# An attention stage in a fused four-layer kernel: keys turned by blocks on VectorE, rotary work on GpSimd, row sums divided out of the output

## The reference

```python
q = rmsnorm(x @ Wq.T).reshape(8, 128, 32, 128)   # 32 query heads, D = 128
k = rmsnorm(x @ Wk.T).reshape(8, 128, 8, 128)    # 8 key heads; each serves 4 query heads
v = (x @ Wv.T).reshape(8, 128, 8, 128)
q, k = rope(q, pos), rope(k, pos)                # halves swapped, times cos and sin
kc, vc = k_cache[block_table], v_cache[block_table]     # 512 cached keys per sequence
p = softmax(q . concat(kc, k) * scale + mask)    # 640 keys per query
x = x + (p @ concat(vc, v)) @ Wo.T
```

## Time and profile before

| | |
|---|---|
| profiled execution, own time | 1516.57 us |
| its span | 1514.8 us (so 1.8 us lie around the span) |
| TensorE matmuls busy | 1422.5 us (94%), 8068 |
| VectorE busy | 1151.0 us (76%), 2779 |
| ScalarE busy | 995.2 us (66%), 1985 |
| GpSimd busy | 495.5 us (33%), 684 |
| mean granted TensorE clock | 0.98 of full speed (2.4 GHz) |
| chain that ended last | TensorE 79% of the span, VectorE 6%, issue 6%, ScalarE 4%, DMA 3% |
| chain, the key transposes L1370 | 2% |
| chain, `attend` L1334 | 13% |

### The profile page before, as it was taken

The page is one execution under the profiler, slowest core; times in us unless marked ns, Lnnn a source line. Parts: engine busy times, 40 slices in busy tenths (PEclk is TensorE's granted clock), DMA queues, the critical chain, the costliest instruction groups (busy, mean ns, idle before and its releaser), DMA issues.

```text
span 1514.8 us, 29533 instructions
## 1 busy us (share of the span) xinstructions
PE 1422.5 (94%) x8068; PEld 1222.2 (81%) x8068; DVE 1151.0 (76%) x2779; ACT 995.2 (66%) x1985; POOL 495.5 (33%) x684
## 2 busy tenths in 40 slices
PE   6989987789999999999999999999999999999888
PEld 4767765678888788888888888888788888888767
DVE  3876666467788788878878887888788878888756
ACT  4756554356677677767767776677677767777643
POOL 5321220144443333334333333333333334333200
PEclk9999999989999999999999999999999999999999
DMA  8885763334321111211211211021111111101214
GB/s 172 299 254 154 220 196 103 112 87 133 113 70 43 51 39 53 61 41 50 62 48 33 71 43 51 29 70 43 51 39 53 61 41 50 63 29 35 98 65 158
DMA packets 103342, 130.47 MB, mean 86 GB/s; under 512 B 11973, under 2 KB 78662, under 8 KB 97782
## 3 DMA queue, kind: packets, MB, share of 16 engines
q1 hardware_dynamic: 97760, 108.96, 23.6%
q0 software_dynamic: 5248, 19.34, 4.7%
q10 hardware_dynamic: 150, 0.01, 0.0%
HBM read 125.11 MB, written 36.72 MB: 107 GB/s over the span
## 4 chain that ended last, share of the span: by engine, by line
PE 79%; DVE 6%; issue 6%; ACT 4%; DMA 3%; POOL 1%; SPq 1%; POOLq 0%; ACTq 0%; DVEq 0%
PE proj_ps L1257 18%; PE sc L1297 14%; PE o_ps L1334 13%; PE proj_ps L1355 12%; PE ring L1316 9%; PE o_ps L1074 3%; PE proj_ps L1074 3%; PE sc L1074 2%; PE ring L1370 2%; PE ring L1382 2%; DMA prep<-scale_dram 1%; DMA wd_raw<-in_WdT 1%; ACT wb L716 1%; ACT prep L665 1%; DVE prep L1621 1%
## 5 line engine op out<-in xcount | busy, mean ns | idle before, releaser
L1814 DVE TENSOR_TENSOR pTl<-ring,pTh 128x512 fp32r<-128x512 f32 x320 | 215.2, 689 | 76.2 <-ACT pTh L900 72.7
L882 ACT ACTIVATE p_sb<-p_sb,bias,rstd 128x640 f32<-128x640 f32 x256 | 235.8, 921 | 48.5 <-DVE bias L1790 48.5
L641 POOL TENSOR_TENSOR rstd<-var,half_neg 128x4 f32<-128x4 f32 x64 | 80.0, 1251 | 524.3 <-DVE var L1851 475.6
L900 ACT ACTIVATE pTh<-ring 128x512 fp32r<-128x512 f32 x320 | 184.4, 599 | 54.5 <-PE ring L1316 53.6
L1780 DVE CUSTOM_DVE_ANT_0 p_sb<-sc,mask 128x640 f32<-128x640 f32 x256 | 209.2, 817 | 6.8 <-PE sc L1297 2.1
L1257 PE MATMUL proj_ps<-wh,xh 128*128 128x512 f32 (+1 forms) x512 | 181.4, 354 | 10.4 <-issue 9.7
L1316 PE MATMUL ring<-ident,p_sb 128*128 128x128 f32 x1280 | 183.7, 275 | 5.1 <-DVE p_sb L1806 3.0
L1316 PEld LDWEIGHTS ring<-ident,p_sb 128*128 128x128 f32 x1280 | 154.3, 142 | 32.6 <-DVE p_sb L1806 3.7
L1257 PE MATMUL proj_ps<-wl,xh 128*128 128x512 f32 (+1 forms) x512 | 173.9, 340 | 0.0
L1257 PE MATMUL proj_ps<-wh,xl 128*128 128x512 f32 (+1 forms) x512 | 173.6, 339 | 0.0
L1297 PE MATMUL sc<-kTh,qTh 128*128 128x320 f32 x512 | 164.5, 321 | 2.5 <-DVE kTl L1915 2.5
(11 more groups left out here) (248 smaller groups left out, 3684.7 us busy)
## 6 DMA issues: line engine op xcount, KB each, us to landing
v_pages<-in_v_cache POOLq DMA_DIRECT2D x128, 128.0 KB, 3.9
k_pages<-in_k_cache SPq DMA_DIRECT2D x128, 128.0 KB, 3.6
k_raw<-k_pages SPq DMA_DIRECT2D x64, 256.0 KB, 3.0
v_raw<-v_pages SPq DMA_DIRECT2D x64, 256.0 KB, 2.9
stage<-in_Wqkv SPq DMA_DIRECT2D x32, 384.0 KB, 3.3
w_raw<-in_WguT SPq DMA_DIRECT2D x19, 512.0 KB, 6.4
stage<-in_WoT SPq DMA_DIRECT2D x32, 256.0 KB, 3.3
w_raw<-in_W3T SPq DMA_DIRECT2D x8, 1024.0 KB, 5.4
```

Source lines behind the costliest of these rows:

```text
L882: act_e.activation(p_sb[:, p_slot(u, h), :], p_sb[:, p_slot(u, h), :], ACT.Exp, bias=bias[:, h:h + 1], scale=rstd[:, u.k % 2, h:h + 1], ac ...
L900: act_e.activation(pTh[:, c, :], ring[c % 2][:, :], ACT.Copy).then_inc(S["pth"], 1)
L1814: v.tensor_tensor(pTl[:, c, :], ring[c % 2][:, :], pTh[:, c, :].bitcast(F32), ALU.subtract).then_inc(S["ptl"], 1)
```

## The change

- The cached keys. `load_k` is now four DMAs that bring the keys in as 128 partitions (32 tokens of a page x 4) so that the 32x32 blocks of the result are transposes of blocks of the source: k_raw is 128x512, its runs in DRAM are 32 floats. VectorE turns all the blocks with one 128x512 `transpose` (`turn_cached_k`, after `low_pt(u-2, 1)`). ScalarE makes the high part from it between `high_pt(u-2, 3)` and `high_pt(u-2, 4)`; the low part moves to GpSimd, behind `k_pow`. `transpose_keys` leaves TensorE.
- Rotary. Both cos products and the key's sum move from VectorE to GpSimd, ahead of the page copies and of `k_pow`; `scale_k` moves to ScalarE, behind `square_q`, as the last piece of its step but the weight splits.
- Softmax. The four `normalise` passes are gone. The row sums' inverses (128x4) are taken at once per unit (`invert`), stored to DRAM (128 stores of 16 B), read back to every partition as a row of 512 (`inv_row`), and `norm_o` on VectorE multiplies o_ps by it in place, after the last `attend` and before `high_o`. `put_inv(u-2)` and `spread_inv(u-2)` stand in SyncE's order behind `load_k(u)` and behind `load_v(u-1)`.
- `bias` is made for two heads at a time (`shift`), after both have their maximum, so `exp` of heads 2 and 3 wait for `mask_max(., 3)`. `high_q` moves ahead of `exp(., 1)`.

```diff
-                sp.dma_start(k_raw[:, :, :], of_head(k_pages, u)).then_inc(k_load, 16)
+                pages = k_pages[u.seq, :, :, :].rearrange("(i r) h d -> r i (h d)", r=PSIZE)
+                for j in range(D // PSIZE):
+                    sp.dma_start(k_raw[j * PSIZE:(j + 1) * PSIZE, :].rearrange("r (i c) -> r i c", c=PSIZE),
+                                 pages[:, :, bass.ds(u.head * D + j * PSIZE, PSIZE)]).then_inc(k_load, 16)
...
+            def put_inv(u):
+                if u.exists():
+                    sp.wait_ge(S["inverted"], u.count(1, 1))
+                    sp.dma_start(inv_dram[u.k % 2], inv[:, u.k % 2, :]).then_inc(S["inv_put"], 16)
+            def spread_inv(u):
+                if u.exists():
+                    sp.wait_ge(S["inv_put"], u.count(16, 16))
+                    sp.dma_start(inv_row[:, :], inv_dram[u.k % 2].rearrange("t h -> (t h)").partition_broadcast(P)
+                                 ).then_inc(S["inv_in"], 16)
...
                 if u.exists() and (u.turn is not None or u.k > 0):
                     load_k(u)
+                put_inv(u + -2)
                 load_in(u + 4, 0)
                 load_out(u + -1, 1)
                 if (u + -1).exists() and (u.turn is not None or u.k > 1):
                     load_v(u + -1)
+                spread_inv(u + -2)
...
+            def turn_cached_k(u):
+                dve.wait_ge(k_load, u.count(4 * 16, 4 * 16))
+                v.transpose(k_turned[:, :], k_raw[:, :]).then_inc(S["kcT"], 1)
+            def norm_o(u):
+                dve.wait_ge(S["pv"], u.count(KC, KC))
+                dve.wait_ge(S["inv_in"], u.count(16, 16))
+                o = o_ps[:, :].rearrange("p (h t) -> p h t", h=REP)
+                v.tensor_tensor(o, o, inv_row[:, :].rearrange("p (t h) -> p h t", h=REP), ALU.mult).then_inc(S["on"], 1)
...
             def high_o(u):
-                act_e.wait_ge(S["pv"], u.count(KC, KC))
+                act_e.wait_ge(S["on"], u.count(1, 1))
```

ScalarE's step:

```diff
+                high_q(u + -1)
                 exp(u + -2, 1)
-                high_q(u + -1)
...
                 exp(u + -2, 3)
-                normalise(u + -2, 1)
-                normalise(u + -2, 2)
...
                 high_pt(u + -2, 3)
+                high_cached_k(u)
                 new_wo(u + -2, 2)
                 high_pt(u + -2, 4)
                 square_q(u)
+                scale_k(u)
                 new_wqkv(u + 1, 1)
-                high_cached_k(u)
                 new_wo(u + -2, 3)
```

TensorE's step:

```diff
                 attend(u + -2, 2)
-                transpose_keys(u)
                 attend(u + -2, 3)
```

VectorE's step:

```diff
                 low_pt(u + -2, 1)
-                cos_q(u)
-                cos_k(u)
+                turn_cached_k(u)
                 low_pt(u + -2, 2)
-                invert(u + -1, 0)
...
                 low_pt(u + -2, 4)
-                sum_k(u)
                 new_wqkv(u + 1, 1)
                 new_wo(u + -2, 2)
-                low_cached_k(u)
                 new_wo(u + -2, 3)
-                scale_k(u)
+                norm_o(u + -2)
                 low_o(u + -2)
```

More of the change, by code:

```diff
@@ L227, in cond_resid_kernel @@
         wol = l1_sb("wol", [P, REP, HID], F32R)
-        k_raw = l1_sb("k_raw", [P, LC, D])
+        k_raw = l1_sb("k_raw", [P, L])
         v_raw = l1_sb("v_raw", [P, LC, D])
@@ L958, in square_k, with scale_k @@
                 if u.back(1):
-                    act_e.wait_ge(S["k_ss"], u.count(1, 0))
+                    act_e.wait_ge(S["q_ss"], u.count(1, 0))
                 act_e.activation(sq_k[:, :], k_sb[:, :], ACT.Square).then_inc(S["k_sq"], 1)
+            def scale_k(u):
+                if not u.exists():
+                    return
+                act_e.wait_ge(S["ksum"], u.count(1, 1))
+                act_e.wait_ge(S["k_pow"], u.count(1, 1))
+                act_e.activation(k_cos[:, :], k_cos[:, :], ACT.Copy, scale=rstd[:, u.k % 2, REP:REP + 1]
+                                 ).then_inc(S["krope"], 1)
             def slot_free(u):
@@ L1357, in output @@
                 i.then_inc(S["y"], 1)
-            def transpose_keys(u):
-                if not u.exists():
-                    return
-                pe.wait_ge(k_load, u.count(16, 16))
-                if u.back(2):
-                    pe.wait_ge(S["ptl"], (u + -2).count(KC, 4))
-                elif u.k == 0:
-                    pe.wait_ge(S["x1l"], HALF)
-                else:
-                    pe.wait_ge(S["knl"], u.count(1, 0))
-                for c in range(LC):
-                    i = nc.tensor.transpose(ring[1][:, c * P:(c + 1) * P], k_raw[:, c, :], ident[:, :])
-                i.then_inc(S["kcT"], 1)
             def transpose_queries(u):
@@ L1886, in low_new_v @@
                                 ).then_inc(S["vnl_set"], 1)
-            def sum_k(u):
-                if not u.exists():
-                    return
-                dve.wait_ge(S["ksin"], u.count(2, 2))
-                dve.wait_ge(S["kcos"], u.count(1, 1))
-                v.tensor_tensor(k_cos[:, :], k_cos[:, :], k_sin[:, :], ALU.add).then_inc(S["ksum"], 1)
-            def scale_k(u):
-                if not u.exists():
-                    return
-                dve.wait_ge(S["ksum"], u.count(1, 1))
-                dve.wait_ge(S["k_pow"], u.count(1, 1))
-                v.tensor_scalar(k_cos[:, :], k_cos[:, :], rstd[:, u.k % 2, REP:REP + 1], None, ALU.mult
-                                ).then_inc(S["krope"], 1)
             def low_q(u):
@@ L1927, in step @@
                 mask_max(u + -1, 1)
+                shift(u + -1, 0)
                 low_pt(u + -2, 0)
                 low_pt(u + -2, 1)
-                cos_q(u)
                 if u.turn is None and u.k == 0:
@@ L1950, in step @@
                 low_q(u)
-                invert(u + -1, 1)
                 low_new_k(u)
@@ L1954, in step @@
                 mask_max(u + -1, 3)
+                shift(u + -1, 1)
                 add_y(u + -2)
```

129 lines of the change are left out of this document (60 added, 69 removed).

## The result

The changed kernel takes 1612.5 us (median of 4 runs, 1607.2 to 1613.7) where the kernel before took 1515.1 on the same chip: ratio 1.0636, 95% interval 1.0611 to 1.066. I had said 1564 and 1500 to 1605. The direction was right, the size was not: 97 us lost instead of 49, above the range.

The account below looks back on a forecast made before the run. It took TensorE's own work to bound the kernel. Span 1514.8 + 3 (middle steps) + 14 (first units) + 32 (heads) = 1563.8 us, so a forecast median of 1564, range 1500 to 1605.

Parts of the forecast that it names:

- The middle steps: Some 50 undisturbed steps in the long middle of the span, each going from 17.28 to 17.35 us: +3 us.
- The first units: First seven units: `k_pow` about 1.3 us later behind four page copies, 2.2 instead of 0.99 from there to `output`: +14 us.
- The gain: Removing `transpose_keys` from TensorE saves 0.44 us per unit over 64 units, 28 us at most; nothing else leaves TensorE.
- the two new waits: TensorE would wait before `attend(., 4)` and before `output`, spending there the 0.44 us per unit it saves.
- the lower bound for `norm_o`: If `norm_o` cost nothing, 0.35 us per step would be won, 18 us over 50 steps.
- rival 1: TensorE keeps its 0.44 us per unit because the chain is shorter or heads cost little: 1487 to 1510, chance 0.17, as 1500.
- Where it goes: From the last probability transposes through `attend`, `norm_o` (0.69), `high_o` and `low_o`, `output` starts 0.07 us later per step.
- My bound of twice 0.69: Upper bound for the length of `norm_o`, which no profile row showed: 35 us lost over 50 steps.
- New heads: Seven times, weight splits ahead of `norm_o`, late keys and the loop's turn cost 4.6 us each: 32 us, bounds 16 and 64.
- Hidden work and the DRAM round trip: Block transpose (0.7 us), GpSimd's added work and the inverses' trip through DRAM cost undisturbed steps nothing; crowded transfers: 1.7 us late.
- rival 3: Key loads in 128 B runs, late inverses or a block transpose over 1.8 us hold up steps: 1592 to 1600 and more, chance 0.17.
- rival 2: The longer chain through `norm_o`, with first-unit and new-head costs, makes the kernel slower, 1530 to 1590 us, chance 0.53.

## Why the prediction was wrong, by its own steps

Two terms of the sum failed. The middle steps were put at +3 us and measured 24, because `norm_o` took 1.09 us and not 0.69. The first units were put at +14 and measured 33, because the sum charged PE's stops alone and put the clock behind them at nothing.

**The gain (0.44 per unit, 28 us at most):** right as a bound, and the two new waits I named are there. Only 0.15 per step remains once the wait before `attend(., 4)` is taken, which comes with the key part itself. My own list of hops had it: the last product of `attend` at 816.15 for 816.29, 0.14 earlier. So the lower bound for `norm_o`, "0.35 per step would be won", was summed wrongly, and rival 1's 1487 was out of reach even with a `norm_o` that costs nothing: 56 steps by 0.15 are 8 us.

**Where it goes (the chain):** the mechanism and every hop were right, one term was mis-sized. `norm_o`, taken at 0.69, the nearest row, measured 1.09. A step of 17.35 became 17.71; with the instruction read in order it was 17.34 to 17.37. Over 56 units that is 24 us instead of the +3 I put down. My bound of twice 0.69 held; I had chosen the wrong place between the bounds, though I had noted that it strides over its operand.

**The first seven units (+14):** 33 measured. `k_pow` came 2.2 us later, not 1.3 (from the start of `copy_q` to that of `k_pow` 10.86 us, before 8.67): the cos product adds only 0.3, the key work 1.0, but the four copies themselves last 4.6 instead of 3.7. The 2.2 from there to `output` was right (2.24). What was missing from the sum altogether is the clock: behind a stop of 3.65 us PE runs at the lower level for 5 us. I charged for the stop alone. The five outputs at the lower level cost 10.8 of the 19 us that I missed; the rest is stops, which come in all seven intervals and not in five and two halves, and the longer `norm_o` there.

The trace has 0.50 behind the stop and 0.43 us from product to product there. The Trainium skill (TensorE: Matmul & The Clock Gate, Part 1) says the same: the throttled state is the default and activity lifts it, and cold products of 512 columns start 426.7 ns apart. It puts the penalty of the ramp below 1% of a typical kernel; here the five outputs pay 10.8 us, 0.7%.

**New heads (4.6 each, 32 us):** 37 us measured: 5.0 each in the six of the middle, more in the last. That is near in sum, and partly by luck. The head's last unit cost 1.9 (I had 1.0; its `norm_o` waits for the split and is 1.07 itself). The Wo unit cost 2.3 (2.2), but not for my main reason: I had the keys 1.3 us late, and VectorE waits for them, once per head as I said, but 0.3 at most. What holds `norm_o` there is the Wo split in front of it, which waits 1.58 for its transfer. The two others named, the new head's first unit and the turn, cost 0.1 or less (0.8 and 0.6), two I had not named 0.3 and 0.4.

**Hidden work and the DRAM round trip:** right in the undisturbed step: transpose 0.70, key runs 2.7 us to landing, `spread_inv` 3.9. The small runs of rival 3 did not decide; only with 4-byte stores did the round trip surface.

**The rivals:** rival 2 was the case, beyond its end of 1590. Its own terms, put right, give 1514.8 + 24 (56 steps) + 33 (first units) + 37 (heads) - 3.7 at the end = 1605, the measured span. The median of all executions stands 5 us above the profiled one, where I had carried over a median 1.8 below it; the profiled execution has a granted clock of 0.972, the three others 0.966 to 0.969. My range ended at 1605, the lower end of rival 3. My own upper bounds for `norm_o` and the heads together would have gone further: 1514.8 + 35 + 14 + 64 = 1628. I had let only one of them err at a time.

## What to carry to other kernels

A pass put on the chain between an accumulation and its consumer costs its length plus its hand-over, less the slack that was there, in every step; so size it by its operands' steps, not by its shape alone. Where an edit makes TensorE stand still as long as in these first units (3.65 us), charge the stop and then the work behind it at the lower clock. And before giving an engine more work, look at what stands in its queue ahead of the instruction that others wait for: here the copies ahead of `k_pow` were worth 1% in the kernel before, more than any part of the change gained.

## What the runs showed of the hardware

- A 128x512 pass with one SBUF operand in 16-byte steps: 1.09 us on VectorE for 0.70 in order, 1.11 on ScalarE for 0.60. Reading and writing PSUM in place cost nothing extra: the 0.70 was in place too, and `low_o`, which only reads PSUM, is 0.69.
- A store of 2 KB in 128 runs of 16 bytes landed after 2.0 us; in 512 runs of 4 bytes the wait for it ended about 9 us after the issue.
- The granted clock was 0.50 behind PE's two stops of 3.65 us in the first units (410.9 to 415.0 us) and 1.00 behind stops filled with products that nobody reads, in the same execution: `output` 5.2 us for 2.8.
- At a loop's turn PE stood still 2.9 us in two pieces in one kernel, 3.0 in one piece in another that differs in where the keys are turned, whatever the DMA runs. The clock fell behind one of six turns and behind five of six. What holds PE there is open.
- A block transpose of 128x512 on VectorE: 0.70 us, like the fp32 subtractions of this size in the same step (0.69).
